# Moving the lower-part subtractions of a cross-attention stage from GpSimd to VectorE

## The chip, the core and the metric

The kernel runs on one core of a Trainium2 chip. A core has five engines with an instruction queue of their own: TensorE (PE), which multiplies matrices into the PSUM banks; VectorE (DVE); ScalarE (ACT); GpSimd (POOL); and SyncE (SP), which issues most of the DMAs. The engines meet only at semaphores. The time is that of the device for one launch, in microseconds.

## What is computed

Two sequences of 2048 rows and 512 columns (x), and a context of 77 rows for each, go through one layer. Everything is in float32:

```python
def _L0_xattn_ref(x, context, ...):
    z = self_attn(x, Wq1, Wk1, Wv1)
    x = layer_norm(x + z, ln1_g, ln1_b)
    z = cross_attn(x, context, Wq2, Wk2, Wv2)
    x = layer_norm(x + z, ln2_g, ln2_b)
    z = jax.nn.relu(x @ fc1_w + fc1_b)
    z = z @ fc2_w + fc2_b
    return layer_norm(x + z, ln3_g, ln3_b)
...
x = x + tanh(g_xattn) * _L0_xattn_ref(_layernorm(x), ctx, ...)
x = x + tanh(g_ffn) * _L0_ffn_ref(_layernorm(x), ...)   # 512 -> 2048 -> 512, silu, weights as 8-bit codes times scales
```

The weights of the attention block are 512 x 512.

## The kernel before

**Split numbers.** TensorE multiplies in the fp32r format, which holds fewer bits than float32. So every operand X is kept as two parts: an upper part hi (X copied to fp32r) and a lower part lo = X - hi. A product is the sum of three passes, hi*hi, hi*lo and lo*hi (PASSES). The upper part is mostly made by ACT (functions hi, hi_...), the lower part by DVE (lo, lo_...), and both must be there before TensorE may start.

**Stages.** The program has three stages: self-attention for both sequences; then the cross-attention stage, with cross-attention, the 512 x 512 two-layer network (fc1, relu, fc2) and the layer norms around them; then the gated feed-forward layer with 2048 units. The change is in the second. It lies at about 690 to 990 us of the profiled execution.

**The cross-attention stage** works on NT = 8 tiles t of 512 rows, each of BT = 4 blocks k of 128 rows. It is a software pipeline: step2(t) does the network of tile t and beside it the cross-attention of tile t+1, and the transposes of tile t+2. The order of the instructions on each engine is written out by hand, in one step2 per engine; an engine does its own list strictly in order, and wait_ge stops all that stands behind it.

PE's list in step2(t): mlp_in(t, 0..3), the products with fc1 for the four chunks f of 128 hidden units, with the transposes of the scores and of the probabilities of tile t+1 between them (turn_scores, turn_probs); cross_values(t+1, 0..3), the products of probabilities and values for four blocks of rows, in PSUM banks 6 and 7 in turn; turn_x1(t+2, ..); mlp_out(t, 0..3), the products with fc2, with turn_x2(t+1, ..) between them. cross_values(t+1, k) waits on z_free until the bank is free, that is for k >= 2 until DVE has done add_z(t+1, k-2).

The hidden units of a chunk f: ACT's relu (L1199) reads the PSUM bank and writes HF2[f % 2]; ACT's hi_hid (L1204) writes the upper part hid2[:, f, 0]; lo_hid writes the lower part hid2[:, f, 1] = HF2 - hi and counts up h_lo. relu(t, f) waits until lo_hid of chunk f-2 has read its buffer. mlp_out(t, 0) waits chunk by chunk on h_lo. In the kernel before, lo_hid stands on POOL (L1413).

POOL's other work in the stage: gain_x2 and bias_x2 (L1425, L1430: the rows N times the gamma, plus a bias, block by block), root_z and root_y (L1400, L1401, L1405: inverse roots of the variances, a few columns each), lo_w (L1420: the lower parts of two units of the third stage's weights per step), and in the step before the last roots_of_x (L1439 to L1445), which waits for statistics by DVE (stats_x3).

DVE's list in step2(t), as far as it matters: add_y(t-1, 3) (L1848); shift_y(t-1, 2) (L1865); softmax(t+1) (L1815 to L1818), after which ACT does the exponential (L1149); sum_probs (L1824, L1825); scale_w (L1903: codes to weights; one per step here, two at t = 6, where a unit's codes must have been loaded); lo_probs (L1525); scale_y and shift_y of block 3 of tile t-1 (L1858, L1865); add_z(t+1, 0..3) (L1836 with an accumulator read, L1840), which reads PSUM and frees the bank; then lo_x1 (L1525), add_y, lo_x2 (L1525) and scale_y and shift_y for the other blocks.

The last step (last_step, t = 7) has no tile behind it. In place of cross-attention it makes the normalized rows of the third stage's first tile: make_factors, h_scale (L2033), h_shift (L2038) and lo_h on DVE, base_x (L1189) and a table load on ACT, and turn_h on PE (L662), where turn_h(0, k) waits for h_shift(0, k).

L652 is the line of every product, L662 that of every 128 x 128 transpose, L1525 that of every lower part made by DVE's helper lo, L1017 that of ACT's helper hi.

Of the kernel before, what the change touches and what calls it, by code (L numbers as in the profile page):

```python
# [20 lines left out]
F32 = mybir.dt.float32  # L21
# [10 lines left out]
C = E // P  # L32
# [162 lines left out]
def build(nc, a, out):  # L195
    ctx = ExitStack()
    with ctx:
# [1132 lines left out]
        def _(pool):  # L1330
# [77 lines left out]
            def root_y(t, k):  # L1408
                root(y_at(t, k), sqE[:, k:k + 1], rsE[:, k:k + 1]).then_inc(rstd2_ready, 1)

            def lo_hid(t, f):
                pool.wait_ge(h_hi, t * C + f + 1)
                nc.gpsimd.tensor_tensor(hid2[:, f, 1, :], HF2[:, f % 2], hid2[:, f, 0, :].bitcast(F32),  # L1413
                                        ALU.subtract).then_inc(h_lo, 1)

            def lo_w(n):

                pool.wait_ge(w_hi, n + 1)
# [36 lines left out]

            def step2(t):
                if t + 1 == NT:
                    lo_hid(t, 0)
                    root_y(t - 1, 3)
                    lo_hid(t, 1)  # L1460
                    gain_x2(t, 2)
                    lo_hid(t, 2)
                    lo_hid(t, 3)
                    gain_x2(t, 3)
                    lo_w(2 * t + 2)
                    bias_x2(t, 2)
                    bias_x2(t, 3)
                    root_y(t, 0)
                    root_y(t, 1)
                    lo_w(2 * t + 3)  # L1470
                    root_y(t, 2)
                    root_y(t, 3)
                    return
                if t:
                    root_y(t - 1, 3)
                gain_x2(t, 2)
                lo_hid(t, 0)
                gain_x2(t, 3)
                lo_hid(t, 1)
                lo_hid(t, 2)  # L1480
                lo_w(2 * t)
                lo_hid(t, 3)
                if t + 2 == NT:
                    lo_w(2 * t + 1)
                for k in range(BT):
                    root_z(t + 1, k)
                if t + 2 == NT:
                    roots_of_x(0)
                bias_x2(t, 2)
                root_y(t, 0)  # L1490
                lo_w(2 * t + 1 if t + 2 < NT else 2 * t + 2)
                bias_x2(t, 3)
                root_y(t, 1)
                gain_x2(t + 1, 0)
                gain_x2(t + 1, 1)
                root_y(t, 2)
                bias_x2(t + 1, 0)
                bias_x2(t + 1, 1)
                if t + 2 == NT:
                    lo_w(2 * t + 3)  # L1500
# [16 lines left out]
        def _(dve):  # L1517
# [291 lines left out]
            def softmax(t):  # L1809

                s = rows(t)
                dve.wait_ge(c_full, t + 3)
                bank = PS[:, 1, 0:BT * SCP].rearrange("p (k n) -> p k n", k=BT)[:, :, 0:SC]
                m = mask2[:, t // TPB:t // TPB + 1, :].to_broadcast([P, BT, SC])
                nc.vector.tensor_tensor(s, bank, m, ALU.add).then_inc(c_free, 1)  # L1815
                dve.wait_ge(c_free, t + 2)
                p2.link(nc.vector.tensor_reduce(mx2, s, AX.X, ALU.max))
                nc.vector.tensor_tensor(s, s, mx2.unsqueeze(2).to_broadcast([P, BT, SC]),  # L1818
                                        ALU.subtract).then_inc(sm_ready, 1)

            def sum_probs(t):

                dve.wait_ge(e_ready, t + 1)
                p2.link(nc.vector.tensor_reduce(sum2, rows(t), AX.X, ALU.add))  # L1824
                p2.link(nc.vector.reciprocal(rc2, sum2))  # L1825
# [17 lines left out]
            def add_y(t, k):  # L1843

                x = N[:, t % 2, k]
                dve.wait_ge(y_full, t * BT + k + 1)
                dve.wait_ge(x2_biased, t * BT + k + 1)
                nc.vector.scalar_tensor_tensor(out=x, in0=PS[:, 4 + k % 2], scalar=1.0, in1=x, op0=ALU.mult,  # L1848
                                               op1=ALU.add, accum_out=sumE[:, k:k + 1]).then_inc(y_free, 1)
                dve.wait_ge(y_free, t * BT + 4 + k + 1)  # L1850
                nc.vector.tensor_scalar(nmuE[:, k:k + 1], sumE[:, k:k + 1], -1.0 / E, None,
                                        ALU.mult).then_inc(mean_ready, 1)

            def scale_y(t, k):

                x = N[:, t % 2, k]
                dve.wait_ge(sq_ready, y_at(t, k))
                return p2.done(nc.vector.scalar_tensor_tensor(out=x, in0=x, scalar=nmuE[:, k:k + 1], in1=vec2[:, 2],  # L1858
                                                              op0=ALU.add, op1=ALU.mult))

            def shift_y(t, k, at):
                p2.wait(at)
                dve.wait_ge(rstd2_ready, y_at(t, k))
                dve.wait_ge(xo_in[k], t * 16 + 16)
                nc.vector.scalar_tensor_tensor(out=xo[:, k], in0=N[:, t % 2, k], scalar=rsE[:, k:k + 1],  # L1865
                                               in1=xo[:, k], op0=ALU.mult, op1=ALU.add).then_inc(xg_ready, 1)
# [43 lines left out]
            def scale_w(n):  # L1910
                q, sc, loaded, times = unit_stage(n)
                scale_codes(q, sc, (loaded, 32 * times))

            def step2(t, kept):


                far = t + 2 < NT
                if t:
                    add_y(t - 1, 3)
                    shift_y(t - 1, 2, kept)  # L1920
                softmax(t + 1)
                sum_probs(t + 1)
                scale_w(2 * t)
                if not far:
                    scale_w(2 * t + 1)
                lo_probs(t + 1)
                if t:
                    at = scale_y(t - 1, 3)
                    shift_y(t - 1, 3, at)
                for k in range(BT):  # L1930
                    add_z(t + 1, k)
                if far:
                    lo_x1(t + 2, 0)
                    lo_x1(t + 2, 1)
                    scale_w(2 * t + 1)
                else:
                    stats_x3(p0, x1b, (x1b_in[0], NT * 16 + 16))
                    scale_w(2 * t + 2)
                add_y(t, 0)
                if far:  # L1940
                    lo_x1(t + 2, 2)
                    lo_x1(t + 2, 3)
                else:
                    scale_w(2 * t + 3)
                add_y(t, 1)
                lo_x2(t + 1, 0)
                at0 = scale_y(t, 0)
                lo_x2(t + 1, 1)
                shift_y(t, 0, at0)
                add_y(t, 2)  # L1950
                at1 = scale_y(t, 1)
                lo_x2(t + 1, 2)
                lo_x2(t + 1, 3)
                shift_y(t, 1, at1)
                return scale_y(t, 2)

            def last_step(t, kept):


                add_y(t - 1, 3)  # L1960
                dve.wait_ge(x3_factors, 1)
                make_factors(0)
                dve.wait_ge(vec3_in, 32)
                dve.wait_ge(w_ready, NT * 2)
                h_scale(0, 0, x1b[:, 0])
                h_scale(0, 1, x1b[:, 1])
                h_shift(0, 0)
                h_shift(0, 1)
                shift_y(t - 1, 2, kept)
                at = scale_y(t - 1, 3)  # L1970
                shift_y(t - 1, 3, at)
                h_scale(0, 2, x1b[:, 2])
                lo_h(0, 0, 0)
                h_scale(0, 3, x1b[:, 3])
                h_shift(0, 2)
                h_shift(0, 3)
                lo_h(0, 0, 1)
                add_y(t, 0)
                scale_w(2 * t + 2)
                lo_h(0, 0, 2)  # L1980
                add_y(t, 1)
                at0 = scale_y(t, 0)
                lo_h(0, 0, 3)
                shift_y(t, 0, at0)
                add_y(t, 2)
                scale_w(2 * t + 3)
                at1 = scale_y(t, 1)
                shift_y(t, 1, at1)
                add_y(t, 3)
                at2 = scale_y(t, 2)  # L1990
                shift_y(t, 2, at2)
                lo_hid3(0, 0)
                at3 = scale_y(t, 3)
                shift_y(t, 3, at3)
# [41 lines left out]
            def h_shift(t, k):  # L2036
                dve.wait_ge(x3_scaled, t * BT + k + 1)
                nc.vector.scalar_tensor_tensor(out=H0[:, k % 2], in0=H0[:, k % 2], scalar=rsH[:, k:k + 1],  # L2038
                                               in1=vec3[:, 1], op0=ALU.mult, op1=ALU.add).then_inc(hn_ready, 1)
# [90 lines left out]
```

## Time and profile before

| | us |
|---|---|
| median of 3 runs | 1710.02 (1709.49 to 1711.75) |
| the profiled execution | 1708.66 |
| its span, first to last instruction | 1706.9 |
| TensorE busy | 1654.9 (97%) |
| VectorE busy | 839.0 (49%) |
| ScalarE busy | 570.1 (33%) |
| GpSimd busy | 361.6 (21%) |

An engine's busy time is the sum of its instructions' records; waiting for a semaphore isn't in it. The records of one engine overlap by some hundredths of a microsecond, so the distance from one start to the next is the better measure of what an instruction costs in a row. In a timeline row, the bracket at the end is the idle time of the engine before the instruction and what released it. The granted clock is the share of TensorE's full 2.4 GHz.

### The profile page before, as it was taken

Reading aid. Unit: us, or ns where it says so; the run is one execution under the profiler, and the core shown is the slowest. Engines: PE = TensorE matmul, PEld = TensorE weight load, DVE = VectorE, ACT = ScalarE, POOL = GpSimd, SP = SyncE. Lnnn points to the kernel's source line nnn. Section 1 sums busy time; section 2 is a strip of 40 time slices with the busy share of each in tenths; the row PEclk is TensorE's granted clock in tenths of the full one; section 3 lists DMA queues with packets and bytes.
Section 4 is the critical chain, followed back from the end, with each engine's and each line's share of the span. In section 5 each row is a group of like instructions: output and inputs, shape, how many; then the busy total and the mean of one; then the engine's idle time right before and its main releaser. Section 6 shows DMA issues by size and latency. Waiting matters only on the chain.

```text
span 1706.9 us, 20645 instructions
## 1 busy us (share of the span) xinstructions
PE 1654.9 (97%) x7734; PEld 1350.7 (79%) x7734; DVE 839.0 (49%) x1720; ACT 570.1 (33%) x990; POOL 361.6 (21%) x562
## 2 busy tenths in 40 slices
PE   6999999999999999799999799999999999999999
PEld 4887888877878888577787588888888888888887
DVE  4666544467564444578888865332223233333311
ACT  3442212125211212456656543232233222232222
POOL 0121110012111100268888820100000000000000
PEclk9999999999999999799999999999999999999999
DMA  6211211132121101734454342101010101010000
GB/s 204 69 56 56 75 38 38 38 105 63 50 81 38 56 19 39 263 124 158 163 171 149 108 149 87 50 0 50 0 50 1 50 0 50 1 42 8 25 1 25
DMA packets 68824, 117.24 MB, mean 69 GB/s; under 512 B 11201, under 2 KB 13249, under 8 KB 68571
## 3 DMA queue, kind: packets, MB, share of 16 engines
q1 hardware_dynamic: 64968, 110.12, 19.9%
q10 hardware_dynamic: 3757, 5.80, 1.1%
q8 instruction: 62, 1.02, 0.2%
q14 instruction: 37, 0.30, 0.1%
HBM read 81.05 MB, written 34.84 MB: 68 GB/s over the span
## 4 chain that ended last, share of the span: by engine, by line
PE 90%; DVE 3%; POOL 3%; ACT 1%; DMA 1%; issue 1%; SPq 0%; DVEq 0%; ACTq 0%
PE banks L652 85%; PE banks L662 3%; PE banks L785 2%; DVE split L1525 1%; DMA plain<-in_L_xattn_Wq 1%; DMA plain<-in_x 0%; ACT split L1017 0%; POOL split L1413 0%; POOL plain L1425 0%; POOL small L1401 0%; POOL plain L1430 0%; DVE plain L1836 0%; POOL split L1420 0%; ACT plain L1095 0%; DVE plain L1565 0%
## 5 line engine op out<-in xcount | busy, mean ns | idle before, releaser
L652 PE MATMUL banks<-split_q,split 128*128 128x512 f32 x2328 | 571.9, 395 | 1.5 <-POOL split L1413 1.4
L652 PE MATMUL banks<-split 128*128 128x512 f32 (+4 forms) x2292 | 550.5, 391 | 13.3 <-DVE split L1525 8.1
L652 PEld LDWEIGHTS banks<-split 128*128 128x128 f32 (+3 forms) x2292 | 417.2, 188 | 114.6 <-issue 14.8
L652 PEld LDWEIGHTS banks<-split_q,split 128*128 128x128 f32 x2328 | 431.9, 189 | 92.7 <-DVE split L1525 2.9
L652 PE MATMUL banks<-split,split_q 128*128 128x512 f32 (+2 forms) x1728 | 394.7, 381 | 5.5 <-DVE split L1525 3.3
L652 PEld LDWEIGHTS banks<-split,split_q 128*128 128x128 f32 x1728 | 306.0, 189 | 61.8 <-DVE split_q L1525 3.3
L1525 DVE TENSOR_TENSOR split<-banks,split 128x512 fp32r<-128x512 f32 (+5 forms) x232 | 146.9, 639 | 176.1 <-ACT split L1017 175.4
L1998 DVE TENSOR_TENSOR split<-plain,split 128x512 fp32r<-128x512 f32 x128 | 88.6, 692 | 258.1 <-ACT split L1317 258.1
L1017 ACT ACTIVATE split<-banks 128x512 fp32r<-128x512 f32 (+5 forms) x232 | 124.5, 556 | 267.7 <-PE banks L785 207.6
L1311 ACT ACTIVATE plain<-banks,small 128x512 f32<-128x512 f32 x128 | 88.0, 688 | 290.2 <-PE banks L652 290.2
L1525 DVE TENSOR_TENSOR split_q<-banks,split_q 128x512 fp32r<-128x512 f32 x68 | 46.8, 689 | 229.2 <-ACT split_q L1017 229.2
L1017 ACT ACTIVATE split_q<-banks 128x512 fp32r<-128x512 f32 x68 | 40.5, 598 | 290.0 <-PE banks L662 204.2
L652 PE MATMUL banks<-split_x,split 128*128 128x512 f32 x444 | 108.9, 393 | 0.0
L1439 POOL TENSOR_TENSOR small<-small 128x4 f32<-128x4 f32 x8 | 1.6, 200 | 488.4 <-DVE small L2017 488.4
L1377 POOL TENSOR_TENSOR plain<-plain 128x512 f32<-128x512 f32 x32 | 41.3, 1289 | 284.4 <-DMA plain<-in_x 280.0
L652 PEld LDWEIGHTS banks<-split_x,split 128*128 128x128 f32 x444 | 82.2, 188 | 21.0 <-DVE split L1998 4.4
L662 PE MATMUL banks<-ident,plain 128*128 128x128 f32 x432 | 69.3, 292 | 23.0 <-DMA plain<-in_L_xattn_Wq 10.8
L662 PEld LDWEIGHTS banks<-ident,plain 128*128 128x128 f32 x432 | 54.2, 149 | 40.5 <-issue 14.8
L1317 ACT ACTIVATE split<-plain 128x512 fp32r<-128x512 f32 x128 | 81.0, 633 | 4.1
L1095 ACT ACTIVATE plain<-plain,small 128x128 f32<-128x128 f32 (+15 forms) x32 | 38.6, 1206 | 107.5 <-DVE small L1703 107.5
L1687 DVE CUSTOM_DVE_ANT_0 plain<-banks,plain 128x512 f32<-128x512 f32 (+2 forms) x72 | 43.4, 602 | 59.9 <-PE banks L652 59.4
L1348 POOL TENSOR_TENSOR small<-small 128x1 f32<-128x1 f32 x64 | 12.7, 198 | 264.6 <-DVE small L1561 264.4
(155 smaller groups left out, 1259.1 us busy)
## 6 DMA issues: line engine op xcount, KB each, us to landing
plain<-in_x SPq DMA_DIRECT2D x64, 256.0 KB, 2.8
xo_scratch<-plain SPq DMA_DIRECT2D x32, 256.0 KB, 2.0
x_scratch<-plain SPq DMA_DIRECT2D x32, 256.0 KB, 2.0
plain<-x_scratch SPq DMA_DIRECT2D x32, 256.0 KB, 2.9
tile_x<-xo_scratch SPq DMA_DIRECT2D x32, 256.0 KB, 3.1
xg_scratch<-tile_x SPq DMA_DIRECT2D x32, 256.0 KB, 2.0
out<-plain SPq DMA_DIRECT2D x32, 256.0 KB, 2.1
tile_x<-x_scratch SPq DMA_DIRECT2D x28, 256.0 KB, 4.3
```

The costliest lines, as they stand in the source:

```text
L652: mm = nc.tensor.matmul(out, left(c, l), right(c, r), start=start and c == 0 and (l, r) == PASSES[0], stop=stop and c == chunks - 1 and (l ...
L662: mm = nc.tensor.transpose(bank[:, c * P:(c + 1) * P], block_of(c), ident[:])
L785: mm = nc.tensor.transpose(PS[:, 2 + n % 2, j * P:(j + 1) * P], Srow[:, i % 2, lo:lo + P], ident[:])
L1017: nc.scalar.activation(dst, src, copy).then_inc(sems[1], inc)
L1095: nc.scalar.activation(Srow[:, i % 2, 0:w], Srow[:, i % 2, 0:w], ACT.Exp, bias=nb[:, i % 2:i % 2 + 1], scale=SCALE, accum_out=rowsum[:, i ...
L1311: nc.scalar.activation(HF3[:, f % 2], PS[:, f % 2], ACT.Silu, bias=b1f[:, f:f + 1]).then_inc(hf3_ready, 1)
L1317: nc.scalar.activation(hid3[f % 2][:, 0, :], HF3[:, f % 2], copy).then_inc(f_hi, 1)
L1348: nc.gpsimd.tensor_tensor(out, var, eps_col, ALU.add).then_inc(eps_added, 1)
L1377: nc.gpsimd.tensor_tensor(x_shifted, xin[:, i % 2], b3_row, ALU.add).then_inc(xo_made, 1)
L1525: nc.vector.tensor_tensor(dst, src, hi_part.bitcast(F32), ALU.subtract).then_inc(sems[1], inc)
L1687: return nc.vector.tensor_tensor_reduce(out=row[:, at + lo_:at + lo_ + n], in0=src, in1=pad[:, at + lo_:at + lo_ + n], scale=1.0, scalar=- ...
L1998: nc.vector.tensor_tensor(hid3[f % 2][:, 1, :], HF3[:, f % 2], hid3[f % 2][:, 0, :].bitcast(F32), ALU.subtract).then_inc(f_lo, 1)
```

## The change

The function lo_hid moves from POOL's program to DVE's, with the same wait, the same operands and the same semaphore. POOL's list of a step loses its four lo_hid; the order of its other instructions stays. DVE's list gets them: in a middle step lo_hid(t, 0) after softmax, lo_hid(t, 1) after the first scale_w, lo_hid(t, 2) ahead of add_z(t+1, 0), lo_hid(t, 3) between add_z(t+1, 0) and add_z(t+1, 1). In the last step they stand after add_y(t-1, 3), after h_shift(0, 0), after h_shift(0, 1) and after shift_y(t-1, 2).

```diff
@@ gpsimd
-            def lo_hid(t, f):
-                pool.wait_ge(h_hi, t * C + f + 1)
-                nc.gpsimd.tensor_tensor(hid2[:, f, 1, :], HF2[:, f % 2], hid2[:, f, 0, :].bitcast(F32),
-                                        ALU.subtract).then_inc(h_lo, 1)
-
...
             def step2(t):
                 if t + 1 == NT:
-                    lo_hid(t, 0)
                     root_y(t - 1, 3)
-                    lo_hid(t, 1)
                     gain_x2(t, 2)
-                    lo_hid(t, 2)
-                    lo_hid(t, 3)
                     gain_x2(t, 3)
                     lo_w(2 * t + 2)
...
                 gain_x2(t, 2)
-                lo_hid(t, 0)
                 gain_x2(t, 3)
-                lo_hid(t, 1)
-                lo_hid(t, 2)
                 lo_w(2 * t)
-                lo_hid(t, 3)
@@ vector
+            def lo_hid(t, f):
+                dve.wait_ge(h_hi, t * C + f + 1)
+                nc.vector.tensor_tensor(hid2[:, f, 1, :], HF2[:, f % 2], hid2[:, f, 0, :].bitcast(F32),
+                                        ALU.subtract).then_inc(h_lo, 1)
+
...
                 softmax(t + 1)
+                lo_hid(t, 0)
                 sum_probs(t + 1)
                 scale_w(2 * t)
+                lo_hid(t, 1)
                 if not far:
                     scale_w(2 * t + 1)
                 lo_probs(t + 1)
                 if t:
                     at = scale_y(t - 1, 3)
                     shift_y(t - 1, 3, at)
-                for k in range(BT):
+                lo_hid(t, 2)
+                add_z(t + 1, 0)
+                lo_hid(t, 3)
+                for k in range(1, BT):
                     add_z(t + 1, k)
...
                 add_y(t - 1, 3)
+                lo_hid(t, 0)
                 dve.wait_ge(x3_factors, 1)
                 make_factors(0)
...
                 h_shift(0, 0)
+                lo_hid(t, 1)
                 h_shift(0, 1)
+                lo_hid(t, 2)
                 shift_y(t - 1, 2, kept)
+                lo_hid(t, 3)
                 at = scale_y(t - 1, 3)
                 shift_y(t - 1, 3, at)
```

## Rows read from the trace of the kernel before

**Rows 1.** the page's chain that ended last: share of the span by engine.
```profile
PE 90%; DVE 3%; POOL 3%; ACT 1%; DMA 1%; issue 1%; SPq 0%; DVEq 0%; ACTq 0%
```

**Rows 2.** busy time in windows: span's window, length, engines, granted clock, DMA.
```profile
801.50:834.00 32.50, 32.27 (x162) 25.93 (x161) 26.84 (x49) 20.49 (x42) 28.00 (x35) 1.00 0.50 162
```

**Rows 3.** waits from 760 to 922 us: engine, line, released by; us, times, longest.
```profile
PE banks L652 <- DVE plain L1836: 1.2, 5, 0.2
ACT plain L1199 <- POOL split L1413: 6.5, 5, 1.3
```

**Rows 4.** PE's waits from 920 to 978 us.
```profile
PE banks L662 <- DVE plain L2038: 4.4, 1, 4.4
PE banks L662 <- DVE split L1525: 2.9, 2, 2.3
PE banks L652 <- DVE split L1525: 1.7, 1, 1.7
PE banks L652 <- POOL split L1413: 1.4, 2, 0.7
```

**Rows 5.** the chain of waits from 920 to 978 us, by line.
```profile
by line: POOL split L1413 13.1%; POOL plain L1425 10.2%; POOL small L1401 9.9%; PE banks L652 9.7%; POOL plain L1430 9.4%; POOL split L1420 8.6%; DVE tile_x L1865 5.8%; issue 5.2%; POOL small L1400 4.8%; DVE plain L2038 4.2%; DVE plain L185
```

**Rows 6.** timeline of PE in one step: start, us, line, shapes, count, idle before.
```profile
805.66 0.50 PE L652 MATMUL banks<-split 77*128 77x512 f32 x1 [0.23 <-DVE plain L1836]
...
806.53 0.73 PE L652 MATMUL banks<-split 77*128 77x512 f32 x2
```

**Rows 7.** timeline of DVE in the same step, same columns.
```profile
797.58 0.47 DVE L1824 TENSOR_REDUCE small<-plain 128x4 f32<-128x308 f32 x1 [0.67 <-ACT plain L1149]
...
799.82 0.68 DVE L1525 TENSOR_TENSOR split<-banks,split 77x512 fp32r<-77x512 f32 x1
800.42 1.17 DVE L1858 SCALAR_TENSOR_TENSOR plain<-plain,small 128x512 f32<-128x512 f32 x1
801.63 1.67 DVE L1865 SCALAR_TENSOR_TENSOR tile_x<-plain,small,tile_x 128x512 f32<-128x512 f32 x1
804.84 0.75 DVE L1836 SCALAR_TENSOR_TENSOR plain<-banks,small,plain 128x512 f32<-128x512 f32 x1 [1.55 <-PE banks L652]
...
805.72 0.75 DVE L1836 SCALAR_TENSOR_TENSOR plain<-banks,small,plain 128x512 f32<-128x512 f32 x1
```

**Rows 8.** two lines' instructions: duration ns min/median/max, first and last start.
```profile
L1998 DVE TENSOR_TENSOR split<-plain,split x128: 678/693/704, 992.4 to 1699.4; 128x512 fp32r<-128x512 f32 x128
L1858 DVE SCALAR_TENSOR_TENSOR plain<-plain,small x26: 744/1474/1784, 759.3 to 968.1; 128x512 f32<-128x512 f32 x26
```

**Rows 9.** POOL in the same step; and all 32 of L1413, ns min/median/max.
```profile
799.30 1.74 POOL L1413 TENSOR_TENSOR split<-plain,split 128x512 fp32r<-128x512 f32 x1
...
L1413 POOL TENSOR_TENSOR split<-plain,split x32: 1277/1480/1741, 731.8 to 969.3; 128x512 fp32r<-128x512 f32 x32
```

**Rows 10.** timeline of DVE and of POOL in the last step.
```profile
964.07 2.44 DVE L2038 SCALAR_TENSOR_TENSOR plain<-plain,small 128x512 f32<-128x512 f32 x2
...
964.53 1.43 POOL L1413 TENSOR_TENSOR split<-plain,split 128x512 fp32r<-128x512 f32 x1
```

**Rows 11.** timeline of ACT in the middle step.
```profile
799.23 0.62 ACT L1204 ACTIVATE split<-plain 128x512 fp32r<-128x512 f32 x1
...
802.62 0.62 ACT L1180 ACTIVATE split<-codes 128x512 fp32r<-128x512 f32 x1
```

**Rows 12.** timeline of DVE in the first step.
```profile
740.03 0.75 DVE L1836 SCALAR_TENSOR_TENSOR plain<-banks,small,plain 128x512 f32<-128x512 f32 x1 [4.34 <-PE banks L652]
```

**Rows 13.** timeline of DVE and of SP's queue in the step before the last.
```profile
946.42 0.69 DVE L1903 SCALAR_TENSOR_TENSOR plain<-plain 128x512 f32<-128x512 int32 x1 [2.91 <-DMA plain<-in_L_ffn_fc_scales]
...
939.57 0.33 SPq L531 DMA_DIRECT2D plain<-in_L_ffn_fc_q  x1
```

**Rows 14.** PE in a window of the last step: length, busy, granted clock, DMA.
```profile
976.00:982.00 6.00, 5.57 (x16) 0.51 0.00 0
```

**Rows 15.** POOL's groups from 926 to 973 us: busy us, mean ns; idle before.
```profile
L1413 POOL TENSOR_TENSOR split<-plain,split 128x512 fp32r<-128x512 f32 x8 | 12.6, 1583 | 0.0
```

## The prediction

> **What bounds the kernel now.** I read the page first: of its span of 1706.9 us the chain of work that ended last lies on TensorE (PE) for 90% and on GpSimd for 3% [rows 1]. So an edit on VectorE (DVE) and GpSimd (POOL) counts only where PE waits for them. Then I cut the cross-attention stage by time. In a middle step PE is busy 32.27 of 32.50 us at full granted clock, DVE 26.84, POOL 28.00 [rows 2]: PE sets the pace, and DVE has about 5.7 us a step free, but not everywhere. The waits of five steps say where: PE waits five times for L1836 (add_z), 0.2 us each, and for nothing else; ScalarE (ACT) waits 6.5 us for POOL's L1413, the instruction moved here, but no PE wait hangs on that one [rows 3]. The end of the stage is different. From 920 us to 978 us its four longest kinds of wait sum to 10.4 us, of which 1.4 us for L1413 [rows 4], and the chain of waits there runs mostly through POOL, with L1413 named first, at 13.1% of it [rows 5].
>
> **The step in detail.** Take the step whose probabilities are summed at 797.58. PE does cross_values 0 and 1 behind the last product; then 2 waits for add_z(0) and begins at 805.66, and the matmuls of cross_values 3 begin at 806.53 [rows 6], 0.81 us after add_z(1) was issued at 805.72 [rows 7]. The same distance holds for add_z(0), issued at 804.84, and cross_values 2 (0.82 us). So the four add_z are a chain with no slack from 804.84 on: each microsecond put between add_z(0) and add_z(1), or ahead of add_z(0) beyond DVE's idle 1.55 us there [rows 7], is a microsecond of PE.
>
> **Durations.** The moved subtraction is 128x512, both inputs and the output in SBUF. The same form on DVE exists later (L1998): 693 ns by the record, 678 to 704 [rows 8], and 0.6 us from one instruction to the next, since records overlap by 0.08 us (799.82 to 800.42) [rows 7]. Where DVE works from SBUF alone while POOL works, both grow: the L1858 of this stage takes from 744 to 1784 ns [rows 8]. The order in which they grow is visible: POOL's L1413 issued at 799.30 takes 1.74 us where the shortest take 1.28 (1.25 us from one to the next, less the overlap of records), and it ends when DVE's L1858 issued at 800.42 (1.17 us) can start its part [rows 7, 9]. They take turns: a DVE instruction that comes while POOL works waits for POOL's whole 1.25 us, and POOL gets its turn even between two DVE instructions in a row. The pair of L2038 at 964.07 shows that: 2.44 us for two, with POOL's L1413 issued at 964.53 getting in between [rows 10]. The Trainium skill (SBUF — State Buffer, "SBUF: two separate sides") says the same more strictly: VectorE instructions with two SBUF inputs and GpSimd compete for one exclusive port pair, and the loser blocks for the whole instruction. By that rule lo_hid(2), below, waits in full; if bandwidth were shared instead, it would not, and the second case below would be the likeliest.
>
> **The change in a middle step (t = 1 to 5).** POOL loses four instructions of 1.25 us and more. DVE gains four of 0.6 us.
> - lo_hid(0), after softmax: DVE waits there 0.67 us for ACT's exponential [rows 7], so its 0.6 us is free.
> - lo_hid(1), after scale_w at 799.85: ACT's record of the upper part ends at 799.85 too [rows 11]. POOL's gain for block 3 now stands where L1413 stood at 799.30, so it works from about 799.8 to 801.0; lo_hid(1) waits for that and ends at 801.5. But scale_y and shift_y, which took 1.17 and 1.67 us [rows 7], now meet an idle POOL: about 0.66 us each by the spacing (0.74 by the record, as the shortest L1858 [rows 8]), and 0.1 us between them. shift_y ends at 803.55 rather than 803.3.
> - lo_hid(2), next: POOL's lo_w(2t) is no longer behind three lo_hid but waits only for ACT's L1180, whose record ends at 802.62 + 0.62 = 803.24 [rows 11]. It asks at 803.3 while shift_y works, gets its turn at 803.55 and holds DVE to 804.8. lo_hid(2) ends at 805.35, and add_z(0) goes from 804.84 to 805.35: +0.5 us. If DVE kept its turn, lo_hid(2) would be done at 804.2, inside the idle 1.55 us: +0.
> - lo_hid(3), between add_z(0) and add_z(1): its source is ready (relu(3) no longer waits 1.3 us for POOL [rows 3], it starts with the end of the product, some 804.1, and the copy ends at 805.4). It takes 0.6 us in the chain without slack: +0.6 us. Nothing on PE covers it.
> I take both, +1.1 us a step, because POOL's request comes 0.2 us and more ahead of DVE's. The bounds: at best the existing 0.2 us of wait goes (-0.2), if the third and fourth subtraction were free; at worst lo_hid(1) to lo_hid(3) cost 1.7 us each less the 1.55 us idle, +3.6 us. Behind the four add_z nothing is late: POOL is ahead, and the products that follow need lo_hid(3) only at their fourth block. The removed 1.29 us wait of ACT was parallel to PE's own product and gives nothing. Five steps: 5.5 us.
>
> **First step.** At t = 0 DVE has no work of a step before and idles 4.34 us ahead of add_z(0) [rows 12]; only lo_hid(3) counts: +0.6 us.
>
> **The last two steps.** At t = 6 both scale_w stand ahead of add_z. With the turns as above lo_hid(1) waits for POOL to 930.65, shift_y for lo_w(12) to 934.25, add_z(0) comes at 935.45, 0.9 us later than now, and lo_hid(3) meets lo_w(13), so that cross_values 3 comes 2.0 us later. But PE then waits anyway, 2.9 us in two waits and 1.7 us, for L1525 [rows 4], behind a DVE that stands 2.91 us for the codes of unit 15 until 946.42 [rows 13]. That load left at 939.57, when SP was free of earlier stores and loads (it had waited 0.2 us for POOL) [rows 13], so a faster lo_w(13) doesn't bring it forward. The 2.0 us disappear in this wait. POOL's four root_z now end early, but its roots_of_x wait for the statistics of DVE (some 943.4) and start within some tenths of a microsecond of where they do now; from there POOL is full to lo_w(15) as before. In the last step DVE does make_factors behind lo_hid(0), which waits for ACT's copy near 959; h_scale(0) then starts some 0.8 us later, and three lo_hid at 0.6 us follow it: 2.6 us. Against that POOL falls idle near 966, and the shift_y, scale_y and shift_y behind them take 0.66 us each where a POOL at work made the like 1.7 us and more [rows 8]: 3 x 1.1 = 3.3 us back. Nearly even; PE stands for turn_h(0,2), the wait for L2038 of 4.4 us [rows 4], about as now; the granted clock is at its low level in the following 6 us (0.51 of 2.4 GHz, that is the 1.2 GHz level, after the idle time [rows 14]) in both. Sum for the end: 0, with -3 us and +2 us as ends.
>
> **Sum.** 0.6 + 5.5 + 0 = 6.1 us on the profiled execution's 1708.66 us: 1714.8 us. The runs' median, 1710.02 us, stands 1.36 us above that execution: 1716.1 us.
>
> **Rivals.**
> 1. Only lo_hid(3) costs: lo_w comes after lo_hid(2) or DVE keeps its turn. 6 x 0.6 = 3.6 us, 1713.6 us. For it: the margin is tenths of a microsecond. Against: the pair of L2038 [rows 10].
> 2. The other side: the end of the stage is POOL's chain [rows 5], eight of the moved instructions lie in it with 12.6 us [rows 15], and PE waits 10.4 us [rows 4]. If these waits are POOL's, 13.1% of 58 us = 7.6 us come back; less 3.6 us in the steps, that is -4 us, 1706 us. It decides once the end gives more than the steps cost. The Trainium skill (GPSIMD Engine Reference, "Engine selection") speaks for this: two-input elementwise work belongs on VectorE, GpSimd being about half as fast. Against: the load, the statistics and ACT's table load, none of them POOL's, stand behind the same waits.
> 3. Nothing measurable: PE's records hide slack and the chain absorbs 0.6 us a step: 1710 us. Against: the 0.81 us distances.
> 4. More turns are lost than I count (+1.8 us a step): +10 us, 1720 us.
>
> **How the numbers follow.** Forecast 0.46, rival 1 0.22, rival 2 0.12, rival 3 0.10, rival 4 0.10. A measurement of this kernel tells about 0.2% (3.4 us) from no change. Slower: 0.46 + half of rival 1 + 0.10 = 0.67. Same: 0.11 + 0.10 = 0.21. Faster: 0.12. The range reaches from rival 3 to rival 4, 1710.0 to 1720.5 us, and leaves out rival 2 and the outer part of rival 4; the forecast's own is 1714 to 1719 us.
>
> **What would show it.** In the profile after: PE's wait for L1836 in a middle step grows from 0.2 us to about 1.3 us and is its only wait there; the subtraction takes 0.69 us as the first and fourth of a step and about 1.7 us as the second and third; middle steps last 33.5 us rather than 32.4; from 920 us on PE's waits, shifted, total about as before. Wrong if the steps keep their length, if the fourth isn't between two waits of PE, or if the wait for L2038 falls below 3 us.

## The result, and the profile after

The changed kernel takes 1725.23 us (median of 4 runs, 1724.21 to 1725.43), against 1710.22 us for the kernel before beside it: ratio 1.0085, interval 1.0068 to 1.0103. It is 15 us slower. I had forecast slower, 6.1 us, with a range to 1720.5 us: the sign was right, the size less than half.

The busy line of the page after. GpSimd lost 44 us (361.6 before); TensorE is busy 10.6 us longer with the same 7734 matmuls:

```profile
PE 1665.5 (97%) x7734; PEld 1359.0 (79%) x7734; DVE 858.2 (50%) x1752; ACT 570.9 (33%) x990; POOL 317.6 (18%) x530
```

PE's waits for the steps 1 to 5, 763.3 to 937.1 us (the line of add_z is L1828 now), which answer to those of [rows 3]:

```profile
PE banks L652 <- DVE plain L1828: 6.2, 10, 0.7
```

Ten waits instead of five, 6.2 us instead of 1.2. One step on PE answers to [rows 6]; the step begins at 831.94:

```profile
845.89 0.97 PE L652 MATMUL banks<-split 77*128 77x512 f32 x3 [0.73 <-DVE plain L1828]
847.35 0.96 PE L652 MATMUL banks<-split 77*128 77x512 f32 x3 [0.49 <-DVE plain L1828]
```

The same step on DVE answers to [rows 7]. L1810 is lo_hid, four times; L1850 and L1857 are scale_y and shift_y:

```profile
836.55 0.69 DVE L1810 TENSOR_TENSOR split<-plain,split 128x512 fp32r<-128x512 f32 x1
...
839.65 1.78 DVE L1810 TENSOR_TENSOR split<-plain,split 128x512 fp32r<-128x512 f32 x1
...
841.95 0.73 DVE L1850 SCALAR_TENSOR_TENSOR plain<-plain,small 128x512 f32<-128x512 f32 x1
842.72 0.75 DVE L1857 SCALAR_TENSOR_TENSOR tile_x<-plain,small,tile_x 128x512 f32<-128x512 f32 x1
843.39 1.78 DVE L1810 TENSOR_TENSOR split<-plain,split 128x512 fp32r<-128x512 f32 x1
845.09 0.73 DVE L1828 SCALAR_TENSOR_TENSOR plain<-banks,small,plain 128x512 f32<-128x512 f32 x1
...
845.94 0.68 DVE L1810 TENSOR_TENSOR split<-plain,split 128x512 fp32r<-128x512 f32 x1
846.54 0.74 DVE L1828 SCALAR_TENSOR_TENSOR plain<-banks,small,plain 128x512 f32<-128x512 f32 x1
```

lo_hid takes 0.69, 1.78, 1.78 and 0.68 us. And POOL, whose L1420 is gain_x2 and whose L1415 is lo_w: lo_w comes at 843.04 while shift_y works, and is served ahead of the third lo_hid:

```profile
837.88 3.00 POOL L1420 TENSOR_TENSOR plain<-plain 128x512 f32<-128x512 f32 x2
843.04 1.58 POOL L1415 TENSOR_TENSOR split<-codes,split 128x512 fp32r<-128x512 f32 x1 [2.16 <-ACT split L1180]
```

So far the forecast. What it lacks is in the length of the steps: PE in the steps t = 0 to 5, from one mlp_in(t, 0) to the next (window, length, PE busy and matmuls, granted clock, DMA share, GB/s):

```profile
727.09:763.30 36.21, 35.49 (x160) 0.91 0.33 103
763.30:796.80 33.50, 32.27 (x162) 1.00 0.50 158
796.80:831.94 35.14, 33.91 (x161) 0.95 0.47 150
831.94:865.44 33.50, 32.27 (x162) 1.00 0.50 158
865.44:901.98 36.54, 35.31 (x162) 0.91 0.45 144
901.98:937.10 35.12, 33.89 (x162) 0.95 0.46 151
```

The first two of the same six steps in the kernel before; the other four are 32.41 us like the second:

```profile
725.68:759.80 34.12, 33.89 (x160) 0.95 0.35 109
759.80:792.21 32.41, 32.18 (x161) 1.00 0.50 163
```

Two of the steps now have the 33.50 us of the forecast, at clock 1.00. The other three middle steps have 1.6 us or 3.0 us more than that, and a lower granted clock. The first step, whose pauses are only 0.23 and 0.49 us, is 2.1 us longer than before. Below, a stretch at the low level of the clock behind a pause is called a fall. The worst step on PE, behind its two pauses:

```profile
879.38 0.96 PE L652 MATMUL banks<-split 77*128 77x512 f32 x3 [0.73 <-DVE plain L1828]
880.84 1.65 PE L652 MATMUL banks<-split 77*128 77x512 f32 x3 [0.50 <-DVE plain L1828]
882.29 1.91 PE L662 MATMUL banks<-ident,tile_x 128*128 128x128 f32 x8
883.85 4.62 PE L652 MATMUL banks<-split_q,split 128*128 128x512 f32 x12
```

and the window of that stretch:

```profile
882.29:888.50 6.21, 6.21 (x23) 0.60 0.52 171
```

Twelve matmuls that take 3.0 us at full clock take 4.62 us; the granted clock of the stretch is 0.60, so it stood at its low level, 1.2 GHz, for most of it. Within one execution the same two pauses are followed by a fall in some steps and by none in others.

The sum of the 16.5 us between the two profiled spans, by the start of mlp_in(t, 0) in each: +1.4 ahead of the first step; +13.8 in the steps 0 to 5 (5.9 of it at full clock, 7.9 by the clock); +1.4 in step 6, where PE waits less in all (3.9 instead of 4.8 us) but has a fall of its own; -1.2 from there to turn_h(0, 3); +1.1 behind it, in code that isn't touched (0.8 us of it up to the third stage's first product, where PE now waits 0.63 us).

### The profile page after: what moved, and what is told of

It is laid out like the page before. It is cut to its first block, busy times and chain, and to the rows that moved or that the text cites. A ratio compares the mean times of both kernels' runs of the same rounds, so it can differ in the third digit from the quotient of the medians.

```text
span 1723.4 us, 20645 instructions
## 1 busy us (share of the span) xinstructions
PE 1665.5 (97%) x7734; PEld 1359.0 (79%) x7734; DVE 858.2 (50%) x1752; ACT 570.9 (33%) x990; POOL 317.6 (18%) x530
## 4 chain that ended last, share of the span: by engine, by line
PE 87%; DVE 6%; ACT 2%; DMA 2%; issue 1%; POOL 1%; ACTq 0%; SPq 0%; DVEq 0%
PE banks L652 82%; PE banks L662 4%; PE banks L785 2%; DVE split L1810 1%; DVE split L1512 1%; DVE plain L1828 1%; DMA plain<-in_L_xattn_Wq 1%; DVE codes L1895 1%; DMA plain<-in_L_xattn_fc_w 0%; ACT split L1017 0%; DMA plain<-in_x 0%; DVE tile_x L1857 0%; ACT plain L1164 0%; ACT plain L1199 0%; ACT plain L1095 0%
## 5 line engine op out<-in xcount | busy, mean ns | idle before, releaser
L662 PEld LDWEIGHTS banks<-ident,plain 128*128 128x128 f32 x432 | 53.9, 148 | 38.0 <-issue 10.7
```

What stands on the lines that cost most here:

```text
L662: mm = nc.tensor.transpose(bank[:, c * P:(c + 1) * P], block_of(c), ident[:])
```

## The experiments

Two theories stood after the comparison. A: the two pauses cost 1.1 us a step, and besides make the granted clock fall. B: the clock falls because of the moved work itself or the load on the chip. Each kernel was timed beside the kernel before; the table gives its median, that of the kernel before beside it, the ratio, and what the steps 1 to 5 last in its profile. A profile shows one execution, and the executions of one kernel differ: those of the kernel before by up to 5.7 us (1705.9 to 1711.6). The profiled one of kernel 2 was the slowest of five (1716.4 to 1721.6), those of kernels 5 and 9 the fastest of five (1713.8 to 1717.5 and 1714.1 to 1718.8).

| kernel | us | before | ratio (interval) | middle steps, us |
|---|---|---|---|---|
| changed | 1725.2 | 1710.2 | 1.0085 (1.0068 to 1.0103) | 33.5, 35.1, 33.5, 36.5, 35.1 |
| 1: lo_hid(3) behind add_z(1) | 1712.1 | 1709.3 | 1.0018 (1.0010 to 1.0027) | 32.9 |
| 2: lo_w behind root_z | 1718.5 | 1710.2 | 1.0052 (1.0039 to 1.0066) | 33.0 or 34.6 |
| 3: both | 1709.5 | 1709.3 | 1.0002 (0.9994 to 1.0011) | 32.4 |
| 4: before, with two pauses | 1731.0 | 1709.3 | 1.0126 (1.0113 to 1.0139) | 35.1 or 36.6 |
| 5: changed, both pauses filled | 1715.2 | 1709.3 | 1.0035 (1.0023 to 1.0047) | 33.5 |
| 6: before, other idle times filled | 1708.2 | 1710.2 | 0.9991 (0.9982 to 0.9999) | 32.4 |
| 7: 3 and 6 together | 1708.4 | 1710.2 | 0.9994 (0.9986 to 1.0003) | 32.4 |
| 8: before, one long pause | 1728.6 | 1710.2 | 1.0108 (1.0093 to 1.0123) | 33.6 to 36.6 |
| 9: changed, first pause filled | 1717.1 | 1709.9 | 1.0043 (1.0029 to 1.0057) | 33.5 |
| 10: changed, second pause filled | 1716.3 | 1709.9 | 1.0039 (1.0027 to 1.0052) | 33.5 |

### The two pauses, one by one (1, 2, 3)

```diff
                 lo_hid(t, 2)
                 add_z(t + 1, 0)
+                add_z(t + 1, 1)
                 lo_hid(t, 3)
-                for k in range(1, BT):
+                for k in range(2, BT):
                     add_z(t + 1, k)
```

> The changed kernel with one instruction moved: lo_hid(t,3) stands behind add_z(t+1,1) instead of ahead of it. Theory A (PE's two waits for add_z cost 0.50 + 0.60 us a step directly, and the pauses make the granted clock fall to 1.2 GHz for some microseconds in some of the steps, together 8 us): the second wait goes, 6 x 0.6 = 3.6 us back; with only one pause a step there are fewer falls of the clock, so 3.6 to 11 us less than the changed kernel, about 1717 us. Rival B (the falls come from the load on the chip, since VectorE and PE are busier together, not from pauses): 3.6 us less, 1721.5 us, and as many slow steps as before.

Measured: 1712.1 us, 13 us less than the changed kernel, for moving one instruction a step by one place. One wait a step is left, and every middle step is at full clock (PE's waits of the steps 0 to 5, and one of the steps):

```profile
PE banks L652 <- DVE plain L1828: 3.9, 6, 0.7
```

```profile
792.70:825.61 32.91, 32.17 (x161) 1.00 0.49 160
```

32.9 us, not 33.5. The 3.6 us that rival B allowed are far exceeded, and so, by 2 us, is the most that theory A gave.

Kernel 2 takes away the other pause instead:

```diff
                 gain_x2(t, 3)
-                lo_w(2 * t)
                 if t + 2 == NT:
+                    lo_w(2 * t)
                     lo_w(2 * t + 1)
                 for k in range(BT):
                     root_z(t + 1, k)
+                if t + 2 < NT:
+                    lo_w(2 * t)
```

> The changed kernel with GpSimd's lo_w(2t) behind the four root_z in the steps up to t = 5; lo_hid(t,3) stays between add_z(0) and add_z(1). Theory A: lo_hid(t,2) takes 0.69 us instead of 1.78, add_z(0) comes on time, the first added wait (0.50 us) goes and the second (0.6 us) stays: middle steps of 33.0 us, and with one longer and one short pause few or no falls of the clock, about 1713 us. Rival B (lo_hid(t,2) is slow for another reason than lo_w): nothing changes, 1725 us.

The third lo_hid takes 0.69 us, and add_z(0) comes with idle time in front of it again:

```profile
843.55 0.69 DVE L1812 TENSOR_TENSOR split<-plain,split 128x512 fp32r<-128x512 f32 x1
844.75 0.75 DVE L1830 SCALAR_TENSOR_TENSOR plain<-banks,small,plain 128x512 f32<-128x512 f32 x1 [0.52 <-PE banks L652]
```

So the 0.5 us were POOL's turn, as the prediction had it. PE pauses 0.23 and 0.48 us. The middle steps without a fall of the clock are 33.0 us, as expected, but in this execution three of the five have one, and the kernel takes 1718.5 us, not 1713:

```profile
832.12:866.74 34.62, 33.91 (x162) 0.95 0.46 152
866.74:899.74 33.00, 32.28 (x162) 1.00 0.49 160
```

Kernel 3 has both edits.

> The changed kernel with lo_hid(t,3) behind add_z(t+1,1), and GpSimd's lo_w(2t) behind the four root_z in the steps up to t = 5, so that it doesn't meet lo_hid(t,2). Theory A: both added waits go in steps 0 to 5, PE waits 0.2 us a step for add_z as in the kernel before, no fall of the clock in these steps, each 32.4 us; 1711 us, with the end of the stage as in the changed kernel (plus or minus 2). Rival B: the waits go but the clock falls in the same steps, some 8 us: 1719 us.

It is the kernel before again, 1709.5 us: 0.2 us of wait a step, 32.4 us, no fall. The moved subtraction costs nothing measurable (at most 1.9 us by the interval's end) where it doesn't stand in the way of add_z, and taking some 46 us from POOL brings nothing.

```profile
PE banks L652 <- DVE plain L1830: 1.4, 6, 0.2
```

```profile
826.87:859.30 32.43, 32.20 (x161) 1.00 0.50 163
```

### Pauses without the change (4, 8)

```diff
                 dve.wait_ge(z2_full, t * BT + k + 1)
+                if t and k < 2:
+                    nc.vector.tensor_scalar(keys[:, 0:(420, 512)[k]], PS[:, 6 + k, 0:(420, 512)[k]], 0.0, None, ALU.mult)
```

> The kernel before, all lo_hid on GpSimd, with an idle VectorE instruction ahead of add_z(t+1,0) (420 columns read from PSUM, about 0.5 us) and one ahead of add_z(t+1,1) (512 columns, 0.6 us); they write to a buffer that nothing reads. Theory A: PE gets about the waits of the changed kernel (0.7 and 0.5 us), and with them the falls of the clock: +6 to +8 us directly and 5 to 10 us by the clock, 1721 to 1727 us. Rival B (the move itself, not the pauses, brings the falls): steps of 33.5 us without falls, 1717 us.

All lo_hid are on POOL, and yet the kernel has the changed one's waits and its falls, a short or a long one in every step:

```profile
814.71 0.97 PE L652 MATMUL banks<-split 77*128 77x512 f32 x3 [0.74 <-DVE plain L1838]
816.18 1.65 PE L652 MATMUL banks<-split 77*128 77x512 f32 x3 [0.51 <-DVE plain L1838]
817.62 1.91 PE L662 MATMUL banks<-ident,tile_x 128*128 128x128 f32 x8
819.18 4.66 PE L652 MATMUL banks<-split_q,split 128*128 128x512 f32 x12
```

and that step whole:

```profile
800.75:837.35 36.60, 35.36 (x161) 0.91 0.46 144
```

1731.0 us, somewhat above what theory A gave (1721 to 1727), and far from rival B's 1717. The pauses alone are enough. Why it has more falls than the changed kernel stays open.

Kernel 8 has two such instructions ahead of add_z(0) and none ahead of add_z(1):

```diff
                 dve.wait_ge(z2_full, t * BT + k + 1)
+                if t and k == 0:
+                    p2.link(nc.vector.tensor_scalar(keys[:, 0:420], PS[:, 6, 0:420], 0.0, None, ALU.mult))
+                    nc.vector.tensor_scalar(keys[:, 0:420], PS[:, 6, 0:420], 0.0, None, ALU.mult)
```

> The kernel before with both idle VectorE instructions (420 columns each) ahead of add_z(t+1,0), none ahead of add_z(1): PE pauses once a step, for about 1.3 us, instead of twice. Theory A1 (the sum of the pauses counts for the clock): about as many falls as with the two pauses, 1722 to 1731 us. Theory A2 (only pauses that come one behind the other with little work between make it fall): steps of 33.5 us at granted clock 1.00, 1717 us.

PE waits once a step, 1.4 us, and the clock falls in four of the five middle steps: 1728.6 us. Theory A2 falls: it takes no second pause. The time lies where A1 put it, but that the sum of the pauses decides isn't shown: kernel 2 has falls with 0.71 us a step in all, kernel 1 none with 0.73 us.

```profile
PE banks L652 <- DVE plain L1839: 8.2, 6, 1.4
```

```profile
799.94:833.51 33.57, 32.21 (x162) 1.00 0.50 157
833.51:870.09 36.58, 35.22 (x161) 0.91 0.44 144
```

### The same pauses with PE at work (5, 9, 10)

```diff
+                if t and k > 1:
+                    for _ in range((3, 2)[k - 2]):
+                        nc.tensor.matmul(PS[:, 0], fc1[:, 0, 0, 0:P], fc1[:, 0, 0, :], start=True, stop=True)
                 pe.wait_ge(z_free, t * BT + B * NB + k + 1)
```

> The changed kernel, with three extra matmuls of 128x512 on PE ahead of cross_values 2 and two ahead of cross_values 3, into bank 0, whose content is not used between; about 0.23 us each, so PE works through most of both pauses. Theory A: PE still loses the 1.1 us a step (filled or idle) but the clock doesn't fall in the middle steps: 1725 - 8 = 1717 us, every middle step 33.5 us at granted clock 1.00. Rival B: more PE work makes it no better: 1725 us or more.

This is the cleanest test: DVE and POOL do what they do in the changed kernel, PE does more, and it is 10 us faster. Every middle step is 33.50 us at clock 1.00, the length that the forecast gave:

```profile
825.90:859.40 33.50, 33.44 (x166) 1.00 0.48 158
```

Against before it is 5.9 us slower (3.9 to 8.0 by the interval), where the forecast's sum was 6.1 us. Kernels 9 and 10 fill one pause each; their edit against kernel 5:

```diff
-                if t and k > 1:
-                    for _ in range((3, 2)[k - 2]):
+                if t and k == 2:          # kernel 9; kernel 10: k == 3, range(2)
+                    for _ in range(3):
```

> The changed kernel with three extra matmuls on PE ahead of cross_values 2 only; the pause ahead of cross_values 3 (0.50 us) stays. Middle steps keep at least 33.5 us. If the falls of the clock hang on the pauses' place (a pause at cross_values 3, as in the kernel with lo_hid(3) alone in the way, which had them): falls in about half of the steps, 1719 to 1722 us. If they hang on the idle time only: 0.5 us a step is less than the 0.73 us that brought none, so no falls, 1716 us.

> The changed kernel with two extra matmuls on PE ahead of cross_values 3 only; the pause ahead of cross_values 2 (0.73 us) stays. As in the kernel with lo_hid(3) behind add_z(1), one pause of 0.73 us a step: no falls, middle steps of 33.5 us, 1716 us. If the falls don't hang on the number of pauses: as in the changed kernel, 1725 us.

Both give 33.5 us a step and no fall in the steps 1 to 5: 1717.1 and 1716.3 us. The first alternative of kernel 9, that a pause at cross_values 3 brings falls in about half of the steps, isn't borne out: the profiled execution has none, and the median lies below the 1719 us that it gave. Filling either pause is enough. Kernel 2 has nearly the same pause at cross_values 3 as kernel 9 (0.48 us) and falls; what it has besides is the 0.23 us ahead of cross_values 2.

PE's waits for add_z in the steps 0 to 5 of kernel 9, then of kernel 10, and one step of each:

```profile
PE banks L652 <- DVE plain L1831: 2.8, 6, 0.5
```

```profile
PE banks L652 <- DVE plain L1831: 3.9, 6, 0.7
```

```profile
825.79:859.30 33.51, 32.98 (x165) 1.00 0.51 157
```

```profile
828.14:861.64 33.50, 32.74 (x163) 1.00 0.51 158
```

### The changed kernel again (11)

> The changed kernel once more, unchanged, for its steps: every middle step 33.5 us plus 0, 1.6 or 3.1 us. If the pattern of long and short steps is the same as in the first profile, it belongs to the program; if it differs with the same sum, it belongs to the moment at which the chip looks. About 1725 us.

One run, 1724.5 us, with the steps 36.2, 33.5, 35.1, 33.5, 36.5 and 35.1 us: the same pattern to a tenth of a microsecond. The last two:

```profile
864.82:901.37 36.55, 35.32 (x161) 0.91 0.45 144
901.37:936.49 35.12, 33.90 (x161) 0.95 0.44 150
```

So in these two executions which steps are hit was not chance; more weren't profiled.

### Looking for a faster kernel (6, 7)

The kernel before has idle times of its own with a low clock behind them: ahead of the first step, and ahead of turn_h(0, 2) [rows 4, 14]:

```profile
725.68 4.57 PE L652 MATMUL banks<-split,split_q 128*128 128x512 f32 x12 [1.61 <-DVE split L1525]
...
977.20 5.18 PE L652 MATMUL banks<-split_q,split 128*128 128x512 f32 x12
```

Kernel 6 fills them:

```diff
+            pe.wait_ge(fcw_lo, C)
             for k in range(BT):
+                fill((0, 0, 4, 5)[k], 5, fc1)
                 turn_x2(0, k)
-            pe.wait_ge(fcw_lo, C)
+            fill(6, 5, fc1)
...
                 if not ahead:
+                    fill(18, 0, fc2)
                     turn_h(0, 2)
```

fill(n, bank, w) is n matmuls of 128x512 from w into a bank that isn't in use.

> The kernel before with extra matmuls of 128x512 in PE's idle times around the stage: four, five and six ahead of turn_x2(0,2), turn_x2(0,3) and mlp_in(0,0), and 18 ahead of turn_h(0,2) of the last step. If the low clock behind these idle times is what the pauses cause, mlp_in(0,0) takes 2.9 instead of 4.6 us and the product behind turn_h(0,2) 2.9 instead of 5.2 us: 4 us less than before, 1705.5 us. If not, 1709 to 1711 us.

Both low stretches go: the first product takes 2.99 instead of 4.57 us, that behind turn_h(0, 2) 3.00 instead of 5.18 us. But only 1.9 us of the 4 arrive, barely clear of nothing, and the profiled execution isn't faster at all (its span is 1707.5 us, 1706.9 before). Its first step starts 1.1 us later, behind a longer stretch at low clock ahead of all extra matmuls, and both gains end in other waits. In step 6 PE waits 3.13 us for a lower part by DVE (1.65 before), and a fall follows: the 48 matmuls behind it take 12.62 instead of 11.45 us. Behind the stage comes a new wait of PE, 2.20 us, which the kernel before doesn't have; ahead of it ACT's first L1318 of the third stage (its silu) comes only at 991.94, right behind the last square_y (L1171), which waited 2.1 us for DVE. PE of kernel 6, then ACT (L921 are the extra matmuls):

```profile
726.77 2.99 PE L652 MATMUL banks<-split,split_q 128*128 128x512 f32 x12
...
955.60 12.62 PE L652 MATMUL banks<-split,split_q 128*128 128x512 f32 x48 [3.13 <-DVE split L1532]
...
972.57 4.28 PE L921 MATMUL banks<-split_q 128*128 128x512 f32 x18
...
977.52 3.00 PE L652 MATMUL banks<-split_q,split 128*128 128x512 f32 x12
...
994.10 3.01 PE L652 MATMUL banks<-split 128*128 128x512 f32 x12 [2.20 <-issue]
```

```profile
991.22 0.72 ACT L1171 ACTIVATE plain<-plain,small 128x512 bf16<-128x512 f32 x1 [2.11 <-DVE small L1858]
...
991.94 0.67 ACT L1318 ACTIVATE plain<-banks,small 128x512 f32<-128x512 f32 x1
```

> The kernel without the two waits (lo_hid(3) behind add_z(1), lo_w behind root_z) with the same extra matmuls. Theory A: as the filled kernel before plus the difference of the two unfilled (0.2 us): 1705.5 us.

1708.4 us, not 1705.5: as kernel 6, within the noise. No version is clearly better than the kernel before.

## Why the prediction had the pauses right and the time 9 us too low

- **The bound, the chain of add_z, the turns:** right, to about 0.1 us. The middle step was forecast at 33.5 us and is 33.50 at full clock; PE's waits 1.23 us a step (about 1.3 forecast); lo_hid 0.69, 1.78, 1.78 and 0.68 us. Kernel 1 and kernel 2 show the two terms separately: 33.5 - 32.9 = 0.6 us for the fourth lo_hid, 33.5 - 33.0 = 0.5 us for the third behind lo_w. Kernel 3 (ratio 1.0002) leaves nothing measurable for the rest of the move.
- **First step:** +0.5 us by its second wait, forecast 0.6; the rest of its +2.1 us is the clock.
- **The last two steps, sum 0:** measured +1.4 in step 6 and -1.2 after it, +0.2 together. In step 6 PE waited 1.16 and 0.92 us for add_z, as worked out, and the later waits took it up. The wait for L2039 (h_shift) is 4.82 us, 4.39 before. That the sum is so near 0 is partly luck: PE's waits shrank from 10.7 to 8.8 us where I had them equal, and the same matmuls took 2.1 us more (51.76 instead of 49.69 us busy), with new falls behind the waits of 1.16 and 1.86 us and a shorter one behind the 4.82 us.
- **The step that failed** is the sentence that each microsecond put into the chain "is a microsecond of PE", and with it the sum of 6.1 us, made at the clock of the kernel before. [rows 14] showed a fall of the clock behind an idle time, and I used it for the 4.4 us wait only and held it equal in both kernels. The missing term, which the sum put at nothing, is 7.9 us in the steps 0 to 5. Kernel 5 puts the two numbers side by side: 5.9 us slower than before with PE kept at work, 15 us with PE idle in the same places.
- **The rivals:** rival 4 had nearly the size (+10 us) but by another mechanism, lost turns, of which there was none more than forecast. Rival 2 (the end of the stage gives back more than the steps cost) fell: the POOL chain lost its eight instructions and the end lasted as long. Rival 1 (3.6 us) and rival 3 (nothing) fell with the two added waits. What the Trainium skill (GPSIMD Engine Reference, "Engine selection") says of elementwise work holds for the instruction: 0.69 us on VectorE against 1.28 us at best on GpSimd; it says nothing of the place. The Trainium skill's rule of the exclusive port pair (SBUF — State Buffer, "SBUF: two separate sides") agrees with kernel 2: the third lo_hid took 1.78 us beside lo_w and 0.69 us without it.

What stays open: what makes one pattern of pauses bring a fall and another none. One pause of 0.73 us a step brought none (kernel 1), nor did a single one of 0.5 us (kernel 9), one of 1.4 us did (kernel 8), and two of 0.23 and 0.48 us did in three of five steps (kernel 2), though they are shorter together than the one of kernel 1. These counts come from one execution each, and the same pauses bring a fall in one step and none in the next: the pauses make falls possible, and what picks the step isn't shown. Places other than these two, and another load of PE around them, weren't tried. The +1.4 us ahead of the first step lies in code that is the same in both; over the other kernels with that same code the first step starts between 724.1 and 728.5 us, so it isn't the change's. The +1.1 us behind the stage wasn't followed up.

## What to carry to other kernels

When PE is the bound at full clock, price a new pause of PE at its length and then ask what the clock does behind it: here 1.1 us of added pauses a step cost 5.9 us by their length, and the kernel lost 15. Look first at what stands between two instructions that free PSUM banks for PE in turn: here 0.6 us there was part of a loss of 15 us, and one place later the whole move cost 2.8 us. A pause that can't be avoided can be filled with matmuls that nobody needs: here five a step gave 10 us back.

## What the runs showed of the hardware

- Pauses of 0.73 and 0.50 us, 1.0 us apart, were followed in three of the five middle steps by a stretch at 1.2 GHz that cost 1.6 or 3.0 us, and in the same three in a second execution.
- With either pause filled by two or three matmuls the clock stayed at 2.4 GHz in all five middle steps of the profiled execution (kernels 9 and 10).
- VectorE instructions with two SBUF inputs and GpSimd's take turns: GpSimd's instruction issued at 843.04 was served between two VectorE instructions that followed one another directly, and the second took 1.78 us instead of 0.69.
